# Turning the unit matrix on TensorE during the load waits at the start of a small vision transformer

## What is computed

```
tokens = einsum('bnd,ed->bne', patches, W) + b       # 32 x 36 x 256
h = concat([cls_tok, cls_token, tokens]) + pos       # 32 x 38 x 256
h = h + attn0(layernorm(h))      # 16 heads, weights 1 + s + s*s/2, causal
h = h + ffn0(layernorm(h))       # one product, both operands rounded to fp4 blocks
h = h + attn1(layernorm(h))      # 16 heads, softmax, causal
h = h + ffn1(layernorm(h))       # low rank: 256 -> 64 -> 1024, gelu, -> 64 -> 256
```

## Time and profile before

| | us |
|---|---|
| median of 3 runs | 307.9 |
| lowest, highest | 306.24, 308.93 |
| the profiled execution | 306.47 |
| its span, first to last instruction | 304.7 |
| TensorE matmul, busy | 258.4 (85%) |
| VectorE, busy | 214.0 (70%) |
| GpSimd, busy | 172.1 (56%) |
| ScalarE, busy | 150.3 (49%) |

### The profile page before, as it was taken

One profiled execution on the slowest core, in us unless ns is written; L12 is line 12 of the kernel. 1 busy time (PEld: TensorE's weight loads), 2 busy tenths in 40 slices (PEclk: granted clock), 3 DMA queues, 4 the chain that ended last, 5 costly groups with the idle time before them and its releaser, 6 DMA issues.

```text
span 304.7 us, 6988 instructions
## 1 busy us (share of the span) xinstructions
PE 258.4 (85%) x2720; PEld 202.9 (67%) x2720; DVE 214.0 (70%) x389; ACT 150.3 (49%) x313; POOL 172.1 (56%) x238
## 2 busy tenths in 40 slices
PE   1679999779998989979689792999999997886983
PEld 1568788557886878868578682788888874432431
DVE  0526557314689999999889999699999995455121
ACT  2212111377988776768155642256555425633440
POOL 7343326224749799797996566676676672245000
PEclk9859999999999999999999997799999999999998
DMA  5899410000000000000000000000000000001011
GB/s 178 192 255 294 110 48 3 0 0 3 2 2 0 4 2 0 3 2 3 2 0 2 0 2 1 3 3 0 2 2 0 2 3 0 3 0 57 4 63 41
DMA packets 9742, 9.87 MB, mean 32 GB/s; under 512 B 4037, under 2 KB 8878, under 8 KB 9710
## 3 DMA queue, kind: packets, MB, share of 16 engines
q1 hardware_dynamic: 9294, 9.42, 11.4%
q10 hardware_dynamic: 416, 0.01, 0.1%
HBM read 8.18 MB, written 1.25 MB: 31 GB/s over the span
## 4 chain that ended last, share of the span: by engine, by line
PE 46%; DVE 30%; issue 7%; POOL 7%; ACT 5%; DMA 3%; SPq 0%; ACTq 0%; POOLq 0%; DVEq 0%
PE psum L1254 10%; PE psum L1290 6%; PE psum L1450 4%; PE psum L1505 4%; DVE img L1007 4%; DVE big L1000 3%; DMA img<-in_x 3%; DVE st L961 3%; DVE big L1092 3%; PE psum L1435 3%; PE psum L1592 3%; PE psum L1580 2%; PE psum L1520 2%; PE psum L1529 2%; DVE xq L1048 2%
## 5 line engine op out<-in xcount | busy, mean ns | idle before, releaser
L1290 PE MATMUL psum<-hnT,a 128*128 128x114 f32 x352 | 48.3, 280 | 1.6 <-ACT mT L681 1.2
L1290 PEld LDWEIGHTS psum<-hnT,a 128*128 128x128 f32 x352 | 43.3, 191 | 6.1 <-ACT mT L681 1.8
L459 POOL TENSOR_SCALAR ve<-mvs 114x1 f32<-114x1 f32 x44 | 19.6, 445 | 42.0 <-DVE mvs L963 40.6
L805 ACT ACTIVATE big<-psum 114x456 f32<-114x456 f32 x44 | 21.8, 552 | 28.6 <-PE psum L1505 28.5
L1254 PE MATMUL psum<-wT,patchT 128*114 128x256 f32 x132 | 32.4, 399 | 1.6 <-DVE patchT L917 0.8
L460 POOL TENSOR_TENSOR rstd<-ve,nhalf 114x1 f32<-114x1 f32 x44 | 31.2, 710 | 3.7
L1092 DVE SCALAR_TENSOR_TENSOR big<-ex,imgmask,z 114x608 f32<-114x608 f32 x33 | 32.1, 1025 | 0.4
L452 POOL TENSOR_TENSOR big<-mT,headmask 128x456 f32<-128x456 f32 x22 | 22.8, 1056 | 15.7 <-ACT mT L651 15.7
L480 POOL TENSOR_TENSOR big<-big,img 114x912 f32<-114x912 f32 x11 | 22.9, 2078 | 14.5 <-ACT big L715 14.5
L1254 PEld LDWEIGHTS psum<-wT,patchT 128*114 128x114 f32 x132 | 24.1, 189 | 7.0 <-DVE patchT L917 2.1
L1000 DVE SCALAR_TENSOR_TENSOR big<-big,img 114x912 f32<-114x912 f32 x11 | 16.7, 1519 | 14.8 <-ACT big L705 14.8
(11 more groups left out here) (158 smaller groups left out, 568.1 us busy)
## 6 DMA issues: line engine op xcount, KB each, us to landing
img<-in_x SPq DMA_DIRECT2D x6, 576.0 KB, 10.3
out<-h_all SPq DMA_DIRECT2D x10, 114.0 KB
w_raw<-in_L_tok_W SPq DMA_DIRECT2D x1, 768.0 KB, 5.7
a_raw<-in_L_attn_Wq SPq DMA_DIRECT2D x1, 256.0 KB, 8.7
a_raw<-in_L_attn_Wk SPq DMA_DIRECT2D x1, 256.0 KB, 8.8
a_raw<-in_L_attn_Wv SPq DMA_DIRECT2D x1, 256.0 KB, 8.9
a_raw<-in_L_attn_Wo SPq DMA_DIRECT2D x1, 256.0 KB, 12.3
qw<-in_L_ffn_weight SPq DMA_DIRECT2D x1, 256.0 KB, 12.5
```

The source lines that it names most:

```text
L805: nc.scalar.activation(pT[:, 4 * g:4 * g + 4, :], PTB[g % 2][0:T, 0:4 * T], ACT.Copy).then_inc(L["p"], 1)
L1290: return nc.tensor.matmul(bk[:, m * T:(m + 1) * T], w[:, c, m * 128:(m + 1) * 128], hnT[:, c, :], start=(c == 0), stop=(c == DC - 1))
```

## The change

TensorE's list gets a helper that turns the unit matrix n times into the first 128 columns of bank 7, in which nothing else is written or read in this stage. It is called with 18 between the wait for the unit matrix and the wait for the weights, with 16 between the weights and chunk 0, and with 5, 10 and 4 after the chunks 1, 3 and 5. No wait, no load and no instruction of another engine changes.

```diff
             pe.wait_ge(consts, 1)
 
+            def keep_clock(n):
+
+                for _ in range(n):
+                    nc.tensor.transpose(bank[7][:, 0:128], ident[:, :], ident[:, :])
+
+            keep_clock(18)
             pe.wait_ge(ld_w, 16)
...
+            keep_clock(16)
             for n in range(KC):
                 turn_chunk(n)
+                if n % 2 == 1:
+                    keep_clock([5, 10, 4][n // 2])
             pe.wait_ge(img_dve, KC // 2)
```

## The result

| | before | after |
|---|---|---|
| median, us | 307.13 | 309.59 |
| lowest, highest | 305.66, 309.28 | 307.76, 311.71 |
| executions | 19 | 19 |
| the profiled execution | 306.47 | 310.66 |
| its span | 304.7 | 308.9 |

The ratio is 1.0073, with a 95% interval from 1.0052 to 1.0093: by the ratio the change makes the kernel 2.2 us slower, and the two medians differ by 2.5. In its code the helper's line is L1211, the weights' turn L1218, the chunks' L1232 and the embedding L1263.

A forecast was written before the change was run, and what follows sets the result against it. TensorE, busy 85% of the span, was taken as the bound, with its first embedding tile at half clock. 306.47 us minus 0.1 gain plus 2.0 clock loss gave 308.4, plus 0.2 offset 308.6; range 305.8 to 311.0.

The forecast's parts named there:

- The prize: First embedding tile: at full clock it starts at 17.75 us for 19.20 and ends at 20.5 for 24.03, 3.5 us sooner.
- Where it ends: Chunk 6, first of the second image half: its load allows no start before 23.92 us; gain 0.1 us, bounds 0 to 0.2.
- The loss: Behind the new 3.4 us wait before chunk 6: the clock falls, costing 2.0 us, between 1.4 and 2.7.
- The first calls: 18 and 16 turns around the weights' transposes: free, VectorE's work moves forward perhaps 0.6 us, all lost again at 13.30.
- The sum: Whole kernel: 306.47 us profiled, minus 0.1, plus 2.0, is 308.4; 0.2 added for the median's offset gives 308.6.
- offset between the median and the profiled execution: Whole kernel: median of the runs shown 307.9 us, 1.4 above the profiled execution; only 0.2 was added.
- That the clock holds: Rival, chance 0.2: same wait before chunk 6, but the clock stays up; only 0.1 us gained, 306.4 to 307.8 us.
- An earlier load: Rival, chance 0.1: the second half's first channel lands earlier than in the trace; gain up to 3.5 us, 303.0.
- Turns at half clock: Rival, chance 0.1: unit-matrix turns don't lift the clock, all 53 take 0.23 us before waiting work; 4.9 us late, 311.4.

## Why the prediction was right

**The prize.** Forecast: chunks at 1.22 us, tile 0 from 17.75 to 20.5. Measured: 1.27 and 1.21 us, 17.94 to 20.8.

**Where it ends.** Forecast: chunk 6 not before 23.92, a wait of 3.4 us, at most 0.2 us of gain. Measured: a wait of 3.52 us, ended by the regrouping, behind a load that this time came 0.35 later. That the load is what cuts the prize off is shown by loading it earlier: then the turns brought 2.5 us between medians of the same chip.

**The loss.** Forecast: 2.0 us, between 1.4 and 2.7. Measured: tile 1 takes 4.45 in place of 2.77, 1.7 us. It is the term that I sized a little too high: the stretch at half clock was 3.4 us long, not 4. That it is the wait and not the turns is shown by filling it (0.9986). The rows that I bounded it by, a wait of 1.85 us that kept the clock and one of 5.55 that didn't, left a wide gap, and the runs fill it from above: waits of 2.19 and 2.23 us were followed by the fall in two profiles.

**The first calls.** I had the 18 and 16 as useful, with 0.6 us lost again at 13.30. Right that all of it is lost. By themselves they make no difference that shows (1.0004); whether they add to the loss beside the other three is open (1.0034 without them, 1.0061 with them on another chip, with overlapping intervals).

**The sum.** Forecast 308.6, within 305.8 to 311.0, and +1.9 us for the change; measured 309.59, and for the change 2.2 us by the ratio (1.6 to 2.9 by its interval) or 2.5 by the medians. The absolute figure was 1.0 too low, and this has two parts of about the same size. I carried only 0.2 of an offset between the median and the profiled execution; I had put it at 1.4 from three executions, and over 19 it is 0.66 (307.13 for 306.47). The other 0.5 us are the change itself. Against the 1.7 us of tile 1 the measured 2.2 to 2.5 leave 0.5 to 0.8 us that no term of the sum stands for. They lie within the interval, so they may be chance; or the later falls come more often with the change. That isn't settled. The forecast also took 1% as what a measurement can tell; with 19 executions of each it told 0.2% either way, so that a loss of 0.7% is clear. (The second low place of the clock line is in slices 25 and 26, where I wrote 24 and 25; nothing rests on it.)

**The rivals.** That the clock holds: it did in the second profiled execution of the change, but only because the wait wasn't there, and not in the median. An earlier load: out here by the measured 23.26, and true as an experiment. Turns at half clock: out in the first profile, where the weights' transposes after the first 18 took 0.17 each and the chunks' 0.10. In the second profile the 18 and the 16 did run at half clock, but the chunks took 0.10 each there too, and chunk 6 came at 23.77, before the 23.92 from which this rival would cost.

## What to carry to other kernels

Before warming an engine up, look at what it will wait for once it is warm: here a DMA that landed at the very moment at which the slow engine arrived, so that speed bought only a wait, and the wait took the clock away where it counted. Warm-up work has to reach up to the next real work, through every wait on the way (30 more dummies took the loss away), and it pays only if the next input is moved forward with it: the same dummies went from 0.7% slower to 0.9% faster when one load was issued ahead of small rows that weren't needed yet.

## What the runs showed of the hardware

Waits of about 2 us cost the clock in one execution and not in another: 2.04 us of work in 4.30 us was followed once by 0.50 and once by 1.00; a wait of 2.19 us was followed by the fall in a profile of a kernel whose median shows no loss. In the profile after, each fall up to 76 us stood for 3.4 us, in which TensorE was busy nearly without a break, and the one at 24.8 us made tile 1 take 1.7 us more (4.45 for 2.77); the profiles with 15 turns in the wait and with only the last three calls have the same 1.7. With 30 turns in the wait, the executions whose mean granted clock was 0.986 or 0.987 took 306.6 us in the median (six), and those at 0.981 took 308.1 (three). Of the 31 executions of the change none had a mean above 0.981.

The granted clock of the first microseconds has to be read from durations. In the second profile of the kernel before the clock is given as 1.00 from 11.2 to 24.0 us, while 24 chunk transposes took 4.45 us, 0.19 each, where they take 0.10 at full clock. In the second profile of the change 16 turns took 3.57 us under a 1.00. So mean clocks compare only between kernels that are alike at the start.

Transposes of the unit matrix alone kept the clock up: 30 of them in the wait, and tile 1 behind them took 2.77 us where it took 4.45 behind the empty wait.

One landing of a DMA can scatter more than the gain that is sought: the embedding weights landed between 6.5 and 6.8 us in thirteen profiles and at 9.05 in one, which hid the new wait in that execution.
